# Expert outputs added to memory by two indirect DMAs per tile instead of one, with a looser order

## What is computed

```python
        out = jnp.einsum('ech,ehd->ecd', hidden, w2) + b2[:, None, :]
        expert_out = out[se, pos] * pw[:, None]
        final = jnp.zeros((T, D), x.dtype).at[pt].add(expert_out)
        return final.reshape(B, S, D)
```

## Time and profile before

| | us |
|---|---|
| median of 3 runs | 887.48 |
| lowest, highest | 884.51, 888.21 |
| span of the profiled execution | 888.4 |

### The profile page before, as it was taken

How to read it: one execution, slowest core, us unless ns; L and a number is a source line. 1 busy time by engine, 2 the same in 40 slices (tenths; PEclk the granted TensorE clock), 3 DMA queues, 4 the chain that set the end, 5 groups by cost and what they waited for, 6 DMA issues and landing times.

```text
span 888.4 us, 15579 instructions
## 1 busy us (share of the span) xinstructions
PE 722.9 (81%) x5500; PEld 545.4 (61%) x5501; DVE 519.8 (59%) x1760; ACT 302.3 (34%) x688; POOL 245.1 (28%) x304
## 2 busy tenths in 40 slices
PE   1888778988777998858798967768868879999993
PEld 1546355566556665647656645745447878988892
DVE  7458677865678774668887367871253443333330
ACT  0133241634333253433353433421334323333330
POOL 5322200470013244001445201330001533333332
PEclk9999899999968999998999997889897989999997
DMA  7950000000001000000111000048001323222220
GB/s 249 412 237 2 0 1 1 19 7 2 1 1 37 23 17 4 2 1 1 54 19 8 1 3 1 25 173 284 0 2 31 63 49 46 36 36 38 36 35 8
DMA packets 29894, 43.63 MB, mean 49 GB/s; under 512 B 5355, under 2 KB 24597, under 8 KB 29830
## 3 DMA queue, kind: packets, MB, share of 16 engines
q1 hardware_dynamic: 19250, 30.87, 10.1%
q0 software_dynamic: 8752, 9.07, 6.3%
q10 hardware_dynamic: 1828, 2.84, 0.9%
HBM read 21.36 MB, written 22.09 MB: 49 GB/s over the span
## 4 chain that ended last, share of the span: by engine, by line
PE 61%; DVE 18%; issue 6%; POOL 4%; ACT 4%; DMA 3%; another core or an unknown queue 1%; ACTq 1%; SPq 1%; DVEq 0%; POOLq 0%
PE qa L1840 26%; PE qc L1840 25%; PE qa L1843 5%; PE qc L1843 4%; DMA out<-qk_T 2%; DVE mx L1435 2%; POOL arena_w L440 1%; DMA mu_row<-in_mu 1%; DVE st L1042 1%; POOL rs_a L475 1%; ACTq L633 1%; DVE arena_e L1256 1%; DVE qk_T L1441 1%; DVE xb L1059 1%
## 5 line engine op out<-in xcount | busy, mean ns | idle before, releaser
L1840 PE MATMUL qc<-arena_w,big 128*128 x468 | 83.1, 328 | 1.4 <-DVE qk_T L1819 1.4
L1840 PE MATMUL qa<-arena_b 128*128 128x128 f32 (+2 forms) x688 | 75.1, 293 | 9.7 <-ACT arena_b L763 4.9
L1840 PEld LDWEIGHTS qa<-arena_b 128*128 128x128 f32 (+2 forms) x688 | 66.1, 195 | 19.4 <-issue 7.5
L1840 PEld LDWEIGHTS qc<-arena_w,big 128*128 128x128 f32 x468 | 75.6, 191 | 2.1 <-issue 2.0
L1008 ACT ACTIVATE big<-qa,arena_b 128x128 f32<-128x128 f32 x156 | 43.1, 375 | 80.8 <-PE qc L1840 66.9
L1840 PE MATMUL qa<-arena_e,nT 128*128 128x192 f32 (+2 forms) x256 | 69.9, 429 | 0.4 <-ACT nT L671 0.3
L1808 DVE COPY arena_b<-qc 128x256 f32<-128x256 f32 x39 | 16.6, 426 | 90.6 <-PE qc L1843 79.6
L603 POOL DMA_INDIRECT out<-qk_T x39 | 61.1, 1566 | 21.0 <-POOL spare L602 10.6
L1840 PEld LDWEIGHTS qa<-arena_e,nT 128*128 128x128 f32 x256 | 47.0, 198 | 22.0 <-issue 12.3
L475 POOL TENSOR_TENSOR rs_a<-rs_a,minus_half 128x4 f32<-128x4 f32 x8 | 8.1, 1012 | 177.5 <-DVE rs_a L1055 170.1
L479 POOL TENSOR_TENSOR rs_b<-rs_b,minus_half 128x4 f32<-128x4 f32 x12 | 12.5, 1042 | 152.3 <-DVE rs_b L1055 152.3
(11 more groups left out here) (368 smaller groups left out, 1592.0 us busy)
## 6 DMA issues: line engine op xcount, KB each, us to landing
slots<-xk SPq DMA_DIRECT2D x1, 13192.0 KB, 43.1
arena_e<-in_w SPq DMA_DIRECT2D x8, 579.0 KB, 7.9
arena_w<-in_w SPq DMA_DIRECT2D x8, 576.0 KB, 9.0
qk_T<-slots SPq DMA_DIRECT2D x39, 97.0 KB, 1.9
out<-hb SPq DMA_DIRECT2D x16, 96.0 KB
arena_e<-in_w_l SPq DMA_DIRECT2D x1, 804.0 KB
arena_e<-in_W ACTq DMA_DIRECT2D x1, 768.0 KB
out<-qk_T POOLq DMA_INDIRECT x39
```

Of the source, the lines that this page charges most:

```text
L1840: return nc.tensor.matmul(o, l, r, start=start, stop=stop)
```

## The change

Each tile's addition becomes two. Every row now carries two output numbers, in columns D + 1 and D + 2. For a row that belongs to its token's lower expert the first is the token's number and the second is outside the output; for a row of the higher expert it is the other way round. The first DMA of a tile (`add_lo`) so adds the rows of lower experts and waits for no earlier addition. The second (`add_hi`) adds the rows of higher experts; it waits for the first DMAs of all preceding tiles and for the second DMA of two tiles before. Landings are counted on four semaphores (lower and higher, even and odd places of the ring), and who waited for `m_add` waits for both a lower and a higher one. The numbers are now computed on DVE in `top_weights` (four instructions per group), from a table of token numbers that lies with the constants; POOL's copy of them (L519) and the load `tok_no` go. Rows are 195 numbers wide in place of 194.

```diff
-XR = D + 2
+XR = D + 3
+        def added(engine, u, turn):
+
+            if not isinstance(turn, int) or turn > 0:
+                for landed in (add_lo, add_hi):
+                    engine.wait_ge(landed[u % 2], turn * (8 * RING) + 16 * (u // 2 - RING // 2 + 1))
...
             for tile in range(EARLY):
                 if tile == EARLY - 2:
                     base_rows(NG - 1)
-                if tile >= RING:
-                    sp.wait_ge(m_add, 16 * (tile - RING + 1))
+                added(sp, tile % RING, tile // RING)
                 slot_load(tile, tile % RING)
...
                 for u in range(RING):
-                    sp.wait_ge(m_add, r * (16 * RING) + 16 * (EARLY - RING + u + 1))
+                    added(sp, u, r + EARLY // RING)
                     slot_load(r * RING + (u + EARLY), u)
...
                 pool.tensor_copy(xk[:, 1, :, 0:D], x6).then_inc(s["keep"], 1)
-                pool.tensor_copy(xk[:, :, :, D + 1].bitcast(I32), bc(tok_no[:, bass.ds(tb * G, G)], 1, 2)).then_inc(s["keep"], 1)
...
+            def add_rows(u, column, landed):
+                pool.indirect_dma_start(
+                    out=rows_out, out_offset=bass.IndirectOffsetOnAxis(ap=xs[:, u, column:column + 1].bitcast(I32), axis=0),
+                    in_=ym[:, u, :], in_offset=None, bounds_check=B * S - 1, oob_is_err=False,
+                    compute_op=ALU.add).then_inc(landed[u % 2], 16)
+
             def add(tile, u, turn):
+
                 pool.wait_ge(m_y, tile + 1)
-                since(pool, carried, tile)
-                since(pool, m_add, tile * 16)
+                since(pool, carried, 2 * tile)
                 pool.tensor_tensor(spare[:, 0:1], minus_half[:, 0:1], minus_half[:, 0:1], ALU.add).then_inc(carried, 1)
-                pool.indirect_dma_start(
-                    out=rows_out, out_offset=bass.IndirectOffsetOnAxis(ap=xs[:, u, D + 1:D + 2].bitcast(I32), axis=0),
-                    in_=ym[:, u, :], in_offset=None, bounds_check=B * S - 1, oob_is_err=False,
-                    compute_op=ALU.add).then_inc(m_add, 16)
+                add_rows(u, D + 1, add_lo)
+                since(pool, add_lo[(u - 1) % 2], turn * (8 * RING) + 16 * ((u + 1) // 2))
+                since(pool, add_hi[u % 2], turn * (8 * RING) + 16 * (u // 2))
+                pool.wait_ge(carried, 2 * tile + 1)
+                pool.tensor_tensor(spare[:, 0:1], minus_half[:, 0:1], minus_half[:, 0:1], ALU.add).then_inc(carried, 1)
+                add_rows(u, D + 2, add_hi)
...
+                inc(T(later[:, 0:3:2, :], bc(i8f[:, :, 0], 1, 2), bc(i8f[:, :, 1], 1, 2), ALU.is_gt), "topk")
+                inc(T(later[:, 1, :], i8f[:, :, 0], i8f[:, :, 1], ALU.is_lt), "topk")
+                w(tb, "topk", 22)
+                for k in range(2):
+                    inc(STT(xk[:, :, :, D + 1 + k].bitcast(I32), later[:, k:k + 2, :], float(NOBODY),
+                            bc(con("tok")[:, tb * G:tb * G + G], 1, 2), ALU.mult, ALU.add), "topk")
...
-            def weight(tile, u):
+            def weight(tile, u, turn):
                 dve.wait_ge(m_down, tile + 1)
-                since(dve, m_add, (tile - (RING - 1)) * 16)
+                added(dve, u, turn)
```

More of the change, by code:

```diff
@@ L46 @@
 for _name, _w in (("ident", 128), ("le", 128), ("lt", 128), ("gt", 128), ("ones", 128), ("iota", KSEL),
-                  ("iota8", NE), ("le8", NE * NE), ("hm", HC), ("cos", HD), ("sin", HD), ("rt", 1), ("t", 1), ("slot", MT)):
+                  ("iota8", NE), ("le8", NE * NE), ("hm", HC), ("cos", HD), ("sin", HD), ("rt", 1), ("t", 1), ("slot", MT), ("tok", B)):
     _C[_name] = (_n, _n + _w)
@@ L75 @@
     ln5=15, x5T=4, x5T_e=2, qk1=6, qk1_e=6, v1p=4, v1=2, lg1=4, mx1=12, lg1T=8, e1=8, pv1=4, pv1_e=4, o1=4, h_l1=12,
-    ln6=15, x6T=4, x6T_e=2, gate=1, smx=5, gexp2=1, topk=20, keep=3, pos=11, counts=1, gatesT_p=4, gatesT=1, b2p=4, out_row=4, base_out=64,
+    ln6=15, x6T=4, x6T_e=2, gate=1, smx=5, gexp2=1, topk=24, keep=2, pos=11, counts=1, gatesT_p=4, gatesT=1, b2p=4, out_row=4, base_out=64,
 )
@@ L94, in build @@
             sem(n) for n in ("route", "scattered", "carried"))
+        add_lo = [sem(f"add_lo{k}") for k in range(2)]
+        add_hi = [sem(f"add_hi{k}") for k in range(2)]
         slot_in = [sem(f"slot_in{u}") for u in range(RING)]
-        m_xT, m_xTe, m_w1, m_up, m_gelu, m_down, m_y, m_add = (
-            sem(n) for n in ("m_xT", "m_xTe", "m_w1", "m_up", "m_gelu", "m_down", "m_y", "m_add"))
+        m_xT, m_xTe, m_w1, m_up, m_gelu, m_down, m_y = (
+            sem(n) for n in ("m_xT", "m_xTe", "m_w1", "m_up", "m_gelu", "m_down", "m_y"))
         slots = nc.dram_tensor("slots", [ROWS, XR], F32, kind="Internal").ap()
@@ L255, in build @@
         ohs = sb("ohs", [128, G, NE])
+        later = sb("later", [128, 3, G])
         tot = sb("tot", [128, G, NE])
@@ L625, in _ @@
             tiles(pool, add)
[L626 removed]
+            all_added(pool)
         @block.scalar
@@ L1106, in _ @@
             dve.wait_ge(setup_v, n)
-            assert step(fill(empty[:, :, D + 1:D + 2].bitcast(I32), NOBODY)) == V_EMPTY
+            assert step(fill(empty[:, :, D + 1:D + 3].bitcast(I32), NOBODY)) == V_EMPTY
             step(fill(gT[64:KR, :, :], 0.0))
@@ L1826, in evacuate @@
                 if more(tile, -1):
-                    weight(tile - 1, (u - 1) % RING)
+                    weight(tile - 1, (u - 1) % RING, turn if u else turn - 1)
             front(0)
@@ L1834, in _ @@
             tiles(dve, evacuate)
-            weight(MT - 1, (MT - 1) % RING)
+            weight(MT - 1, (MT - 1) % RING, (MT - 1) // RING)
         @block.tensor
@@ L2499, in _constants @@
         cos=np.repeat(np.cos(ang), 2, axis=-1), sin=sin, rt=np.float32(1) / (p + 1).astype(np.float32), t=p + 1,
-        slot=np.tile(np.arange(MT), (128, 1)))
+        slot=np.tile(np.arange(MT), (128, 1)), tok=np.arange(B)[None, :] * S + np.arange(S)[:, None])
     return np.concatenate([np.asarray(parts[n], np.float32) for n in _C], axis=1)
```

19 lines of the change are left out of this document (9 added, 10 removed).

## The result

| | before | after |
|---|---|---|
| median, us | 886.0 (4 runs) | 905.0 (4 runs) |
| lowest, highest | 884.35, 888.21 | 902.65, 906.56 |
| span of the profiled execution | 888.4 | 904.4 |
| its mean granted clock | 0.931 | 0.901 |

The ratio is 1.021, 95% interval 1.019 to 1.023: slower by 19 us, about 2%. The forecast of 890.8 was wrong, and so was its range (886 to 900).

What follows compares the result with a forecast made beforehand. PE's work and DVE's weight copy were taken as level bounds in the expert loop; 1.4 (copy) + 0.5 (routing) + 1.4 (tail) = +3.3 on the median 887.48 gave 890.8 us, range 886 to 900.

Steps and rivals of the forecast that it cites:

- Second addition, POOL's unit: Expert loop, POOL: a second addition of 1.56 us per tile, unit 1.95; the pair fits the 4.73 us tile, hidden.
- rival on POOL: Expert loop: POOL becomes the bound, a pair of additions takes 5.02 us, over 4.73; 899 us in all; chance 0.18.
- the blocked copy: Expert loop, DVE: the weight copy waits for the running addition's end, 33 us lost, 922 in all; chance 0.10.
- Copy beside the DMA: Expert loop, DVE: weight copies meeting the higher addition lose 0.08 us each, on the path for 17 tiles, +1.4 us.
- Who waits for the second landing: Slot loads and queue around the last scatters: waits for higher additions are hidden or taken up by POOL's idle time, 0.
- first rival: The rival in which POOL becomes the bound of the expert loop, 899 us; chance 0.18.
- Routing: Four DVE instructions per group: +0.5 us in the last group; in the three joint stages covered, at most 3 x 0.5.
- Tail: From tile 36 POOL is the bound, its additions end at 881.15 in place of 879.78, +1.4 us.
- Base: Stages before 680 us: nothing but four short instructions per group changes; a different time there would spoil the sum.

Runs made afterwards that it cites:

- e5: Kernel before with the new start-up alone (token numbers with the constants, their own load gone): 885.48 us, ratio 0.9995.
- e1: Kernel after with the old start-up (8 KB load of token numbers back, TensorE and VectorE wait for it): 904.21 us, ratio 1.019.
- e19: Kernel before with the four routing instructions at the place of after, results not read, on a quiet chip: 894.17 us, ratio 1.005.
- e20: Kernel before with the same four instructions behind the computation of the slots, results not read, on a quiet chip: 885.45 us, ratio 0.9985.
- e14: Kernel after, unchanged, run again on the chip of the padded kernels: 904.19 us, ratio 1.020 to before.
- the padding: Kernel after with 48 matmuls that nobody reads added in the last group's attention: 897.89 us, ratio 1.010 to before.
- e15: Kernel after with padding, late routing instructions, POOL's changed order, and second additions of tiles 2 to 5 cut to 16 rows: 894.25 us, ratio 0.9945.

## Why the prediction was wrong

- **Second addition, POOL's unit.** Right: 78 DMAs, most of 1.56 (mean 1.58), a unit of 1.94 (forecast 1.95), 0.22 to 0.79 us idle left before a lower addition in the loop. Neither rival on POOL or the blocked copy came, in the loop.
- **Copy beside the DMA, +1.4.** Nearly right in sum, not in detail: 25 tiles take 114.7 in after and 113.6 in the quiet kernels with one addition, +1.1. But it is 6 copies at up to 0.18 in place of 17 at 0.08; the others inside a DMA lose nothing. Against the profiled before it would read as 0. The rule in the Trainium skill ("SBUF — State Buffer", "Who interferes with whom"), that one excludes the other for the whole instruction, had been priced at 33 us; the trace does not bear it out here: at 818.21 the copy ran inside the DMA and lost nothing, at 823.17 it lost 0.18.
- **Who waits for the second landing, 0.** Wrong by 5.4 to 6.9 us. The step "the loads of tiles 9 and 10 slip by as much, and PE comes to them later still" fails: tile 10's load is 3.9 us late for PE. The 7.01 us idle that were to take up the queue are not the kernel's own. They had been opened in the profiled before by halts of DVE at tile 7 and behind it, which no profile of a quiet chip has. The first, in DVE's timeline of before, and the idle time before tile 5's addition in POOL's of e5:

```profile
707.51 0.43 DVE L1808 COPY arena_b<-qc 128x256 f32<-128x256 f32 x1 [6.44 <-remote]
...
719.08 0.19 POOL L600 TENSOR_TENSOR spare<-minus_half 128x1 f32<-128x1 f32 x1 [2.13 <-DMA out<-qk_T]
```

  In e5 2.13 us were there for the 5.9 that the prediction put into the queue. After's tiles 4 to 6 are closer together than the profiled before's, and POOL, with 1.95 us more for each, meets them with its queue full. That is the first rival's mechanism at one place.
- **Routing, +0.5, joints covered.** The 0.5 of the last group was right (0.4: tile 2's weighting). "Covered" was wrong, and is the failed step with the largest share: 9 to 11 us for the 0 charged. "PE takes it at 566.58: covered" took PE to need only the first of the two instructions behind the row of 1.17. It starts 0.05 behind the end of the second (565.36 + 1.17 = 566.53), and in e5 and e1 it moved with that one, by 0.36. By itself that is 1.1 us in three stages. But it lies in a stretch at the lower clock, and the clock then stays low longer behind each joint, and in the attention after the last: 9 to 11 us from four instructions of 0.16 to 0.25 us. Why so small a delay holds the clock down, no run shows; that the place of the four decides it, e19 and e20 do. No rival of the prediction had the clock in it, though the page's row of granted clock was there to read.
- **Tail.** Right: +1.3 for +1.4 (1.1 to 1.8 against e5 and e19). Not foreseen: from the end of the last addition to the end of the span all kernels with two additions take 6.2 to 6.3 us (after 904.4 - 898.13), all with one 8.5 to 8.6 (888.4 - 879.78).
- **Base.** The last sentence, that a different time before 680 us "would spoil the sum without touching its steps", named the case and gave it no chance and no width. It should have had both.

The sum from e5 to after again: 11.2 before tile 0, 5.4 to tile 13, 1.1 to tile 38, 1.1 in the tail, -2.3 behind: 16.5, the difference of the spans (885.1 and 901.6), on two quiet chips. The forecast had 0.5, 0, 1.4, 1.4 and 0.

## What to carry to other kernels

Read the granted clock before pricing an edit: where stretches at the lower clock stand next to the edited place, a delay of 0.4 us on TensorE's path is not worth 0.4 us, and its price has to be bounded by how long those stretches may grow. Small instructions of another engine go behind the ones that TensorE waits for, and a stage in which it runs in short pieces at the lower clock can be worth filling with matmuls that nobody reads. An idle time that is to take up a new load must be the kernel's own, in more than one execution. And a term that reads as 0 between two single profiles may be the reference's own delay: here profiles of kernels with one addition on quiet chips turned 0 into 1.1 us in the loop, and a gain of 0.9 among the first tiles into a loss of 5 to 7.

## What the runs showed of the hardware

- TensorE stayed at 1.2 GHz for 37.5 us (653.4 to 690.9 in e14); from 654 to 687 it had no idle time over 0.80 us and was busy 24.7 of 33. The Trainium skill, "TensorE: Matmul & The Clock Gate", "HAM oscillation — how this bites in real kernels", describes kernels that fall back to the lower clock because of long waits for DMAs in each round. The return to it again and again is seen here (22 stretches in after before 870 us); long waits are not, in this stretch: they were for DVE and ACT, 0.5 to 0.8 us each. What lets the clock rise again was not tried beyond the padding.
- Chips differ. On three, before kept within 4.0 to 7.2 us over 19 executions each; on the fourth it went from 887.7 to 907.9, with clocks of 0.900 to 0.935.
- An indirect DMA of 16 rows holds POOL 1.34 us (e15), one of 128 rows 1.56. A weight copy of DVE that began 0.09 to 0.41 us into one lost nothing, one that began 0.67 to 0.72 us into it lost up to 0.18, and the DMA 0.15 (after, 27 of 28 copies). Why the moment counts is open.
- DVE can halt for 4 us with all it waits for in place (before's profile at 707.51: PE's transposes had ended at 703.63). All eight profiles on the unquiet chip have an idle time of over 5 us at the same tile, put down to "remote"; the ten on the quiet ones have none. Its cause stays open, and so does the cause of the 2.3 us at the end of the span.
